# Two 16-head attentions: probabilities normalised before they are turned, and values as the stationary operand on 64-column tiles

## The reference, cut to what matters

```python
# layer 1 (layer 2: no norm of q and k, but hidden keys)
q = (emb @ Wq.T).reshape(B, SQ, 16, 64).transpose(0, 2, 1, 3)   # k, v from context
q = _layernorm(q, qn_w, qn_b); k = _layernorm(k, kn_w, kn_b)
attn = softmax(einsum('bhqd,bhkd->bhqk', q, k) * scale, axis=-1)
# layer 2: attn = where(mask[:, None, None, :], -inf, attn) before softmax
out = einsum('bhqk,bhkd->bhqd', attn, v)
out = out.transpose(0, 2, 1, 3).reshape(B, SQ, 16 * 64) @ Wu.T + bu
# x = x + tanh(g_xattn[layer]) * out
```

## Time and profile before

| | |
|---|---|
| time, median of 3 runs | 1562.96 us (1562.08 to 1563.18) |
| the profiled execution | 1561.37 us, its span 1559.6 us |
| attention 1, from first projection to its last L144 | 166.4 to 483.0 us |
| attention 2, the same | 664.7 to 947.0 us |
| busy, whole span | PE 87%, PEld 67%, DVE 54%, ACT 46%, POOL 9% |
| mean granted TensorE clock | 0.922 of 2.4 GHz |

### The profile page before, as it was taken

The page is one execution under the profiler, slowest core; times in us unless marked ns, Lnnn a source line. Parts: engine busy times, 40 slices in busy tenths (PEclk is TensorE's granted clock), DMA queues, the critical chain, the costliest instruction groups (busy, mean ns, idle before and its releaser), DMA issues. The chain is left out here.

```text
span 1559.6 us, 26943 instructions
## 1 busy us (share of the span) xinstructions
PE 1352.5 (87%) x8843; PEld 1045.2 (67%) x8843; DVE 845.7 (54%) x2280; ACT 710.9 (46%) x1593; POOL 146.7 (9%) x256
## 2 busy tenths in 40 slices
PE   6766799999996899689999997984699987999995
PEld 5642477777775487578888886973477764766664
DVE  4549777777763554645555553346687762122224
ACT  4331676776762302245555552442355542333343
POOL 1010000000001000000000002005244421000000
PEclk9869899999996999889999997995699987999998
DMA  8000000000000000000000004002000000000000
GB/s 335 1 1 0 1 1 1 1 1 2 1 1 1 1 1 0 1 1 1 2 1 2 1 1 115 8 1 108 1 1 1 0 1 1 1 1 1 1 1 28
DMA packets 6427, 24.52 MB, mean 16 GB/s; under 512 B 797, under 2 KB 1311, under 8 KB 5418
## 3 DMA queue, kind: packets, MB, share of 16 engines
q1 hardware_dynamic: 6314, 23.03, 4.3%
HBM read 21.98 MB, written 1.05 MB: 15 GB/s over the span
## 5 line engine op out<-in xcount | busy, mean ns | idle before, releaser
L1317 DVE SCALAR_TENSOR_TENSOR XN<-bank,gate,XN 128x128 f32<-128x128 f32 x256 | 89.8, 351 | 224.8 <-PE bank L1281 222.2
L1297 ACT ACTIVATE e_hidden<-bank,small 128x512 f32<-128x512 f32 x152 | 104.4, 687 | 214.6 <-PE bank L1269 214.5
L767 PE MATMUL bank<-a_va,a_pT 128*128 128x65 f32 x1024 | 129.4, 269 | 0.8 <-ACT a_pT L933 0.5
L1281 PEld LDWEIGHTS bank<-attention_weights,e_hidden 128*128 128x128 f32 x1024 | 119.2, 192 | 14.8 <-issue 14.8
L767 PEld LDWEIGHTS bank<-a_va,a_pT 128*128 128x128 f32 x1024 | 124.4, 192 | 2.3 <-ACT a_pT L933 0.8
L1019 DVE TENSOR_REDUCE a_mx<-bank 128x4 f32<-128x512 f32 x128 | 87.8, 686 | 64.9 <-PE bank L807 64.4
L1269 PE MATMUL bank<-XNT,attention_weights 128*128 128x512 f32 x256 | 121.2, 606 | 1.2 <-PEq L541 1.2
L1281 PE MATMUL bank<-attention_weights,e_hidden 128*128 128x128 f32 x1024 | 119.3, 275 | 0.0
L933 ACT ACTIVATE a_pT<-bank 128x512 f32<-128x512 f32 x128 | 76.6, 599 | 41.8 <-PE bank L840 41.8
L1027 DVE TENSOR_TENSOR a_shifted<-bank,a_mx 128x512 f32<-128x512 f32 x128 | 88.3, 690 | 3.4
L1912 PEld LDWEIGHTS bank<-blk_va,blk_pT 128*128 128x128 f32 x512 | 64.5, 194 | 33.5 <-issue 21.9
(11 more groups left out here) (353 smaller groups left out, 2646.3 us busy)
## 6 DMA issues: line engine op xcount, KB each, us to landing
attention_weights<-in_a SPq DMA_DIRECT2D x2, 2048.0 KB, 11.7
mod_ring<-in_mod_weights SPq DMA_DIRECT2D x4, 576.0 KB
ctx_both<-in_ctx SPq DMA_DIRECT2D x1, 2048.0 KB, 9.2
attention_weights<-in_up SPq DMA_DIRECT2D x1, 2048.0 KB, 8.2
attention_weights<-in_down SPq DMA_DIRECT2D x1, 2048.0 KB, 12.7
down<-in_down SPq DMA_DIRECT2D x1, 1536.0 KB, 18.2
down<-in_mod_weights SPq DMA_DIRECT2D x2, 576.0 KB
X<-in_x SPq DMA_DIRECT2D x4, 256.0 KB, 3.9
```

The lines of the kernel that those rows point to most:

```text
L767: last = pe.matmul(value_bank[:, j * (W + 1):(j + 1) * (W + 1)], pT[:, i.slot(2), j * 128:(j + 1) * 128], va[:, p, g // 2 * 8 + 2 * j + g ...
L1281: last = pe.matmul(down_bank[j][:, 0:width], layer[0:rows, f, j * 128:(j + 1) * 128], down(g, f), start=f == 0, stop=f == NB - 1)
L1297: act.activation(hidden[0:rows, p, f, :], up_bank_of(i, f)[0:rows, :], function, bias=up_bias(g, f)).then_inc(hidden_ready, 1)
L1317: dve.scalar_tensor_tensor(out=total, in0=down_bank[j][:, e * D:(e + 1) * D], scalar=gate_column(k, 4 * q + j, g * per_group + e), in1=tot ...
```

## The change

Between the exponential and `turn_p` two steps come in: VectorE sums each head's exponentials and inverts the sum (`total_up`), GpSimd multiplies the probabilities by it (`normalise_p`). The turned probabilities are thus normalised. In `values` the operands swap: a head's 64 value columns are stationary, the turned probabilities are moving, and the two heads of a pair write to partitions 0 to 63 and 64 to 127 of a bank by column tiles. Two items are done at once, in slots of odd items, and the bank holds the output already turned. `invert_sums`, `normalise_o` and `turn_o` go. `keep_o` copies 512 columns every second item. `pT` has four buffers. The lags move as the first hunk shows.

```diff
     if qk_norm is not None:
         lag = {"square": 1, "turn_qk": 2, "keep_qk": 3, "scores": 6, "project_v": 6, "subtract": 6, "exponentials": 7,
-               "turn_p": 8, "keep_p": 8, "values": 10, "turn_o": 12, "out": 12, "normalise": 13, "turn_x": 13}
+               "sums": 7, "turn_p": 9, "keep_p": 9, "values": 11, "keep_o": 11, "out": 12, "normalise": 13, "turn_x": 13}
     else:
-        lag = {"keep_qk": 1, "scores": 4, "project_v": 4, "subtract": 4, "exponentials": 5,
-               "turn_p": 6, "keep_p": 7, "values": 8, "turn_o": 10, "out": 10, "normalise": 11, "turn_x": 11}
+        lag = {"keep_qk": 1, "scores": 4, "project_v": 4, "subtract": 4, "exponentials": 5, "sums": 5,
+               "turn_p": 7, "keep_p": 8, "values": 9, "keep_o": 10, "out": 11, "normalise": 12, "turn_x": 12}
...
-        va, oT = sb("va", [128, 2, H, W + 1]), sb("oT", [128, 2, 8 * 128])
-        shifted, probs, pT = sb("shifted", [128, 2, 512]), sb("probs", [128, 2, 512]), sb("pT", [128, 2, 512])
-        mx, rec, on = sb("mx", [128, 2, 4]), sb("rec", [128, 2, 4]), sb("on", [128, 2, 4, 2, W])
+        va, oT = sb("va", [128, 2, H, W]), sb("oT", [128, 2, 8 * 128])
+        shifted, probs, pT = sb("shifted", [128, 2, 512]), sb("probs", [128, 2, 512]), sb("pT", [128, 4, 512])
+        mx, total, rec, pn = sb("mx", [128, 2, 4]), sb("total", [128, 2, 4]), sb("rec", [128, 2, 4]), sb("pn", [128, 2, 512])
...
-            pool.memset(va[:, :, :, W:W + 1], 1.0).then_inc(cleared, 1)
-
-            def body(at):
-                b = at(0)
+            def normalise_p(i):
+                m, p = i.number, i.slot(2)
+                await_count(pool, inverted, m + 1)
+                if i.older_than(2):
+                    await_count(pool, p_turned, m - 1)
+                pool.tensor_tensor(pn[:, p, :].rearrange("p (h s) -> p h s", h=4),
+                                   probs[:, p, :].rearrange("p (h s) -> p h s", h=4),
+                                   rec[:, p, :].unsqueeze(2).to_broadcast([128, 4, S]), ALU.mult).then_inc(p_normed, 1)
+
+            def body(at):
+                if at(0).number == 0:
+                    stage_qk(batch_of(at(0)))
+                if at(-2).alive and at(-2).offset % 4 == 0:
+                    stage_qk(batch_of(at(-2)))
+                if at(1).alive and at(1).offset % 4 == 0:
+                    stage_v(batch_of(at(1)))
+                if at(lag["sums"]).alive:
+                    normalise_p(at(lag["sums"]))
+            sweep(pool, G, 8, depth, body, rolled=False)
...
-                if i.older_than(1):
-                    await_count(pe, o_normed, m)
+                if i.older_than(2):
+                    await_count(pe, o_kept, m // 2)
                 for j in range(4):
-                    last = pe.matmul(value_bank[:, j * (W + 1):(j + 1) * (W + 1)],
-                                     pT[:, i.slot(2), j * 128:(j + 1) * 128], va[:, p, g // 2 * 8 + 2 * j + g % 2, :],
-                                     start=True, stop=True)
-                last.then_inc(weighted, 1)
+                    for a in range(2):
+                        last = pe.matmul(value_bank[64 * a:64 * a + 64, j * 128:(j + 1) * 128],
+                                         va[:, p, g // 2 * 8 + 2 * j + a, :],
+                                         pT[:, (i.offset - 1 + a) % 4, j * 128:(j + 1) * 128],
+                                         start=True, stop=True, tile_position=(0, 64 * a))
+                        if j == 3:
+                            last.then_inc(weighted, 1)
...
-            def turn_o(i, at):
-                await_count(pe, o_normed, i.number + 2 - i.offset % 2)
-                await_out_bank(at)
-                for j in range(2):
-                    last = pe.transpose(out_bank[:, j * 128:(j + 1) * 128],
-                                        on[:, i.offset // 2 % 2, 2 * (i.offset % 2) + j, :, :].rearrange("p a w -> p (a w)"),
-                                        k.ident)
-                last.then_inc(o_turned, 1)
...
-                await_out_bank(at, ("turn_o",))
-                await_count(pe, o_kept, i.number + 1)
+                n = i.number // 4
+                await_count(pe, o_kept, 2 * n + 2)
+                if n:
+                    pe.wait_ge(norm.kept, n)
...
-                await_count(pe, exped, m + 1)
+                await_count(pe, p_normed, m + 1)
...
-                if at(lag["turn_o"]).alive:
-                    turn_o(at(lag["turn_o"]), at)
-                if at(lag["values"]).alive:
+                if at(lag["values"]).alive and at(lag["values"]).offset % 2 == 1:
...
-                await_count(act, o_turned, m + 1)
-                if g == 0 and i.older_than(8):
+                await_count(act, weighted, m + 1)
+                if g == 1 and i.older_than(8):
                     await_count(act, y_done, b - 1)
-                act.activation(oT[:, p, g * 256:(g + 1) * 256], out_bank[:, 0:256],
-                               ACT.Copy).then_inc(o_kept, 1)
+                act.activation(oT[:, p, g // 2 * 512:g // 2 * 512 + 512], value_bank[:, :], ACT.Copy).then_inc(o_kept, 1)
...
-                if i.older_than(2):
-                    await_count(act, weighted, m - 1)
-                act.activation(pT[:, p, :], turn_bank[i.slot(turns)][:, :], ACT.Copy).then_inc(p_kept, 1)
+                if i.older_than(4):
+                    await_count(act, weighted, (m - 4) // 2 * 2 + 2)
+                act.activation(pT[:, i.slot(4), :], turn_bank[i.slot(turns)][:, :], ACT.Copy).then_inc(p_kept, 1)
...
-                if at(lag["turn_o"]).alive:
-                    keep_o(at(lag["turn_o"]))
+                if at(lag["keep_o"]).alive and at(lag["keep_o"]).offset % 2 == 1:
+                    keep_o(at(lag["keep_o"]))
...
-            def invert_sums(i):
+            def total_up(i):
                 m, p = i.number, i.slot(2)
-                await_count(dve, weighted, m + 1)
-                dve.reciprocal(rec[:, p, :], o[:, :, W:W + 1].rearrange("p h w -> p (h w)")).then_inc(inverted, 1)
-
-            def normalise_o(i):
-                m, p = i.number, i.slot(2)
-                await_count(dve, inverted, m + 1)
-                if i.older_than(4):
-                    await_count(dve, o_turned, m - 2 - i.offset % 2)
-                dve.tensor_tensor(on[:, i.offset // 2 % 2, :, i.offset % 2, :], o[:, :, 0:W],
-                                  rec[:, p, :].unsqueeze(2).to_broadcast([128, 4, W]),
-                                  ALU.mult).then_inc(o_normed, 1)
+                await_count(dve, exped, m + 1)
+                dve.tensor_reduce(total[:, p, :], probs[:, p, :].rearrange("p (h s) -> p h s", h=4), AX.X,
+                                  ALU.add).then_inc(totalled, 1)
+                await_count(dve, totalled, m + 1)
+                if i.older_than(2):
+                    await_count(dve, p_normed, m - 1)
+                dve.reciprocal(rec[:, p, :], total[:, p, :]).then_inc(inverted, 1)
...
-                if at(lag["values"]).alive:
-                    invert_sums(at(lag["values"]))
+                if at(lag["sums"]).alive:
+                    total_up(at(lag["sums"]))
...
-                if at(lag["values"]).alive:
-                    normalise_o(at(lag["values"]))```

TensorE in attention 1, three slots in a row (even, odd with `output`, then the head of the next even one); a_on is the attention output before turning, a_oT after. Before:

```order
L807 MATMUL bank<-a_kT,a_qT 128x128 x8
L788 MATMUL bank<-consts,a_on 128x128 x2
L767 MATMUL bank<-a_va,a_pT 128x65 x4
L831 MATMUL bank<-attention_weights,a_cv 128x512
L840 MATMUL bank<-consts,a_probs 128x128 x4
L853 MATMUL bank<-attention_weights,a_cs 128x512
L780 MATMUL bank<-consts,a_qn 128x128 x4
L788 MATMUL bank<-consts,a_on 128x128 x2
L767 MATMUL bank<-a_va,a_pT 128x65 x4
L819 MATMUL bank<-attention_weights,a_oT 128x128 x8
```

More of the change, by code:

```diff
@@ L704, in stage_head_attention @@
         qT, kT = sb("qT", [128, 2, 8 * 128]), sb("kT", [128, 2, 8 * 128])
-        va, oT = sb("va", [128, 2, H, W + 1]), sb("oT", [128, 2, 8 * 128])
-        shifted, probs, pT = sb("shifted", [128, 2, 512]), sb("probs", [128, 2, 512]), sb("pT", [128, 2, 512])
-        mx, rec, on = sb("mx", [128, 2, 4]), sb("rec", [128, 2, 4]), sb("on", [128, 2, 4, 2, W])
+        va, oT = sb("va", [128, 2, H, W]), sb("oT", [128, 2, 8 * 128])
+        shifted, probs, pT = sb("shifted", [128, 2, 512]), sb("probs", [128, 2, 512]), sb("pT", [128, 4, 512])
+        mx, total, rec, pn = sb("mx", [128, 2, 4]), sb("total", [128, 2, 4]), sb("rec", [128, 2, 4]), sb("pn", [128, 2, 512])
         if qk_norm is not None:
             sq, ssq, qn = sb("sq", [128, 512]), sb("ssq", [128, 2, 8]), sb("qn", [128, 2, 512])
-        staged, v_staged, cleared = sem("staged"), sem("v_staged"), sem("cleared")
+        staged, v_staged = sem("staged"), sem("v_staged")
```

(22 more changed lines are left out.)

1 line of the change is left out of this document (removed).

## The result

The changed kernel takes 1510.87 us (median of 4 runs, 1509.63 to 1512.01), before 1562.52: ratio 0.967, 95% interval 0.9653 to 0.9686. The forecast was 1505 us, range 1490 to 1557. The profiled span fell from 1559.6 to 1510.2 us. Attention 1, from its first projection to its last L144, went from 316.6 to 284.5 us, attention 2 from 282.3 to 266.7. The other stages took 1.7 us less together, which is not explained by anything here.

What follows compares the result with a forecast made beforehand. TensorE was taken to bound both attentions. Gains of 38 us in attention 1 and 20 in attention 2, together 58, off the profiled 1561.4 gave 1503.5; the median lies 1.6 above, so 1505 us, range 1490 to 1557.

Steps and rivals of the forecast that it cites:

- TensorE as the bound: TensorE bounds both attentions (94.17 and 99.08 of 100 us); 0.98 us `turn_o` and 3.36 us old `values` leave per batch.
- A: The forecast itself: column tiles run beside each other, 1505 us, own range 1490 to 1520; chance 0.62.
- V: TensorE time of two new `values` for two items each, per batch; each 16 instructions, forecast 1.05 us.
- B: Column tiles in `values` take turns, V = 1.9 us, total 1553 us; chance 0.14.
- C: Loads of 64 stationary columns in `values` lie open, V = 2.75 us, total 1604 us; chance 0.10.
- Waits in the odd slots: TensorE waits once per batch: 0.79 us before attention 1's scores; 0.5 and, behind `output`, 0.9 before attention 2's projections.
- The pace of attention 1: A batch of four items in attention 1 falls from 18.54 to 16.1 us.
- Rival D: VectorE bounds attention 1, or attention 2's waits add up in a chain; paces 17.0 and 15.9, 1526 us; chance 0.14.
- My 0.2 us for VectorE's density: Added to attention 1's pace: with VectorE busy 14.8 of 15.92 us, not every wait can be hidden.
- GpSimd at nothing: GpSimd's four products and copies, 5.1 of 16.1 us a batch in attention 1, were costed at nothing.
- Ends: Head and tail: attention 1 saves about 1 and 5 us; attention 2's output starts 2 later, its tail saves 7.
- The pace of attention 2: A batch of four items in attention 2 falls from 16.36 to 15.2 us.

Runs made afterwards that it cites:

- e1: Changed kernel with, in `values`, all four matmuls of the first column tile before the four of the second: 1537.51 us, ratio to before 0.9841.
- e8: Changed kernel with only the norm's two ScalarE steps moved behind exponential and `keep_qk`; L135 and L140 stay: 1496.81 us, ratio to before 0.9577.
- e5: Changed kernel with the edits of e2 and e3 together: 1462.25 us, ratio to before 0.9357.
- e4: Changed kernel with GpSimd's product done twice per item, once into a spare buffer: 1517.59 us, ratio to before 0.9709.
- e7: Changed kernel with the product with the reciprocals done by VectorE, GpSimd only staging: 1578.44 us, ratio to before 1.0105.
- e2: Changed kernel with the norm's ScalarE steps behind exponential and `keep_qk`, L135 at its slot's end, L140 a slot later: 1487.09 us, ratio to before 0.9509.
- e3: Changed kernel with two PSUM banks for attention 2's q and k projection, one for `turn_p`, `keep_p` a slot earlier: 1486.43 us, ratio to before 0.9514.

## Why the prediction was right, and what was off

- **TensorE as the bound, `turn_o` and the old `values` removed.** Right. 49.4 us of span went; 58 were forecast. The case that came true is A.
- **V.** Forecast 1.05 from the row tiles, measured 1.03; e1 shows that it rests on the two tiles being served beside each other. By the Trainium skill's rule on weight loads (TensorE: Matmul & The Clock Gate, The mechanism) loads of the same row group would lie open, the end that I had priced at 2.75. The trace gives 1.03, so here they do not. B and C fall. Even tile by tile V is 1.51, below the 1.95 from which I had forecast a loss.
- **Waits in the odd slots.** Before scores in attention 1 0.79 forecast, 0.71 measured, the first half of which TensorE already spends ahead of the turn; in attention 2 0.5 and 0.9 forecast, 0.56 and 0.93 measured.
- **The pace of attention 1, 16.1: mis-sized by 0.77 us.** The working held the norm's steps in ScalarE's queue for attention 2 only. In attention 1 they hold up `keep_qk` and so v's projection by 1.18 us a batch, 15.3 us in 13 batches; e8 gets 15.5 us back. Rival D's first half, VectorE as the bound by its total time, did not come true: it is busy 0.8425 x 17.06 = 14.4 us a batch (14.8 forecast), and in e5 90.39 of 100 with TensorE at 97.54. What counted was where the update stands in its queue. My 0.2 us for VectorE's density stood in the place of that wait.
- **GpSimd at nothing.** Right for one product: TensorE's loads waited for it 3.6 us in all, and in e4 even two products came in time. What e4 lost is the overlap with VectorE's L135. e7 is 67.6 us slower than the changed kernel, some 20 of them by the lower clock.
- **Ends.** Attention 1: head 47.7 to 44.8 us (1 less forecast, 2.9 measured), tail from output 13 to the end 27.9 to 20.5 (5 less forecast, 7.5 measured). Attention 2: head + 3.5 (+ 2), tail - 7.0 (- 7).
- **Sum.** 32.1 us in attention 1 (38 forecast), 15.6 in attention 2 (20). The pace of attention 1 missed by 10 us, its ends gave 4.3 more than forecast: the total is nearer than its terms, and that part is luck.
- **The pace of attention 2, 0.23 us above 15.2.** The steady batch fell from 16.40 to 15.55 us, 0.85 where 1.14 were forecast. Start to start, the four projections of q and k (L860) take 0.25 us more than before, because one that had to wait takes 1.06 us instead of 0.99 or 0.89, and the two of v 0.10 more; the waits took 1.50 instead of 1.40; `output` gave back 0.08 and V 0.05. In the mean of 13 intervals the shorter last one hides 0.08 of it.
- **One reading was too strong.** That loads are busy 73 to 89 of 100 us does not say that all of it lies under matmuls: with TensorE at 94.17 and 99.08 it is at least 67.5 and 87.7.

## What to carry to other kernels

When a step leaves a slot, look at what it covered: here the removed `turn_o` and `values` exposed chains of projection, copy and bank. Moving a short step of another chain behind the urgent copy (e2, 23.8 us) and giving the bank a twin (e3, 24.4 us) were together worth nearly as much as the change itself (48.6 us against 51.7). A step that waits for a far engine should not stand at the head of a queue whose next entries are ready. An engine at 63% busy need not have room for more; what counts is what stands behind the new instruction in its queue (e7), what runs beside it on another engine (e4: 0.35 us became 1.17), and whether TensorE's clock holds (e7).

## What the runs showed of the hardware

Two 64-column float32 tiles, alternating, took 1.03 us for 16 instructions of 128 moving columns, against 0.98 to 1.10 us for row tiles and 1.51 us for the same instructions tile by tile. The load of 64 stationary columns lasts 137 ns where that of 128 lasts 192:

```profile
L774 PEld LDWEIGHTS bank<-a_pT,a_va x1024: 132/137/138, 202.5 to 893.2; 128*64 128x64 f32 x171
```

GpSimd's product of 128x512 took 1039 ns beside a VectorE busy 84 of 100 us, as it did before beside other work. Two meetings cost time: VectorE's L135 took 1.17 us instead of 0.35 while GpSimd's second product ran (e4), and in e7, where TensorE stood 2.6 us once a batch, its granted clock was 0.93 from 300 to 400 us, against 1.00 in the changed kernel with waits of 1.1 us.
